# SyncE's row transfers in another order, and the self-attention row after the first search round of its half slot

## The reference, cut to what matters

```
x1 = x  + causal self-attention(LN(x))      16 heads of 32, q and k normed per head
x2 = x1 + cross-attention(LN(x1), ctx)      keeps the 32 largest of 512 scores per row and head
y  = x2 + MLP(LN(x2))                       512 -> 2048 -> 512, int8-like activations, ternary weights
```

## Time and profile before

| | |
|---|---|
| median of 3 runs | 3952.01 us (3951.01 to 3952.15) |
| the profiled execution | 3955.8 us |
| its span, first to last instruction | 3954.0 us |
| mean granted TensorE clock | 0.86 of full speed |
| busy share: TensorE, VectorE, ScalarE, GpSimd | 84%, 81%, 62%, 48% |

### The profile page before, as it was taken

How to read it: one execution, slowest core, us unless ns; L and a number is a source line. 1 busy time by engine, 2 the same in 40 slices (tenths; PEclk the granted TensorE clock), 3 DMA queues, 4 the chain that set the end, 5 groups by cost and what they waited for, 6 DMA issues and landing times.

```text
span 3954.0 us, 61337 instructions
## 1 busy us (share of the span) xinstructions
PE 3320.5 (84%) x18502; PEld 2447.8 (62%) x18502; DVE 3219.5 (81%) x7571; ACT 2451.1 (62%) x4921; POOL 1916.0 (48%) x2444
## 2 busy tenths in 40 slices
PE   2587788998989989998989898998999898877765
PEld 1355576766666667666766676766766676555542
DVE  4311199999989999899989898899979998999961
ACT  3343466666766667666866676667766676555533
POOL 0123234446655465546654555445654564355435
PEclk7667888988989989988988898988898898887778
DMA  8112332332222222322222222322232221211100
GB/s 277 50 51 57 98 77 69 81 86 66 71 66 77 66 62 77 97 76 62 78 78 78 70 67 63 84 72 68 78 82 79 73 70 41 62 46 35 33 22 19
DMA packets 167443, 283.04 MB, mean 72 GB/s; under 512 B 40639, under 2 KB 52939, under 8 KB 166606
## 3 DMA queue, kind: packets, MB, share of 16 engines
q1 hardware_dynamic: 160782, 275.98, 25.6%
q10 hardware_dynamic: 6336, 3.15, 0.3%
HBM read 113.27 MB, written 31.46 MB: 37 GB/s over the span
## 4 chain that ended last, share of the span: by engine, by line
DVE 38%; PE 28%; POOL 13%; issue 9%; ACT 5%; SPq 3%; DMA 1%; DVEq 0%; POOLq 0%; ACTq 0%
DVE cW L881 17%; DVE top L876 14%; PE bank L682 6%; PE bank L607 5%; PE bank L654 4%; POOL srs L1147 3%; SPq L513 3%; PE bank L593 2%; POOL hh L1111 2%; DVE smx L1013 2%; PE bank L670 2%; PE bank L635 2%; POOL hh L1115 2%; PE bank L694 2%; PE bank L701 2%
## 5 line engine op out<-in xcount | busy, mean ns | idle before, releaser
L881 DVE MATCH_REPLACE8 cW<-top,cW 128x512 f32<-128x512 f32 x1536 | 1026.3, 676 | 0.0
L876 DVE MAX8 top<-cW 128x8 f32<-128x512 f32 x1536 | 980.8, 680 | 0.0
L797 ACT ACTIVATE PT<-bank 128x512 f32<-128x512 f32 (+3 forms) x1024 | 539.6, 527 | 363.5 <-PE bank L593 359.8
L1168 POOL TENSOR_TENSOR cS<-cS,cW 128x512 f32<-128x512 f32 x512 | 641.7, 1275 | 199.3 <-ACT cW L825 198.8
L607 PE MATMUL bank<-cv,PT 128*128 128x33 f32 x4096 | 589.0, 291 | 113.3 <-ACT PT L797 111.8
L607 PEld LDWEIGHTS bank<-cv,PT 128*128 128x128 f32 x4096 | 559.1, 211 | 148.1 <-ACT PT L797 141.6
L607 PEld LDWEIGHTS bank<-sv,PT 128*128 128x128 f32 x2560 | 404.8, 214 | 81.1 <-ACT PT L797 57.4
L1175 POOL TENSOR_SCALAR cnb<-top 128x2 f32<-128x2 f32 x256 | 49.0, 191 | 807.4 <-DVE top L876 793.1
L593 PE MATMUL bank<-ident,cS 128*128 128x128 f32 x2048 | 352.2, 300 | 82.4 <-POOL cS L1168 82.4
L825 ACT ACTIVATE cW<-cW,cnb 128x512 f32<-128x512 f32 x512 | 347.6, 733 | 118.5 <-DVE cW L881 118.1
L607 PE MATMUL bank<-sv,PT 128*128 128x33 f32 x2560 | 377.0, 282 | 37.2 <-ACT PT L797 36.0
(11 more groups left out here) (151 smaller groups left out, 6105.0 us busy)
## 6 DMA issues: line engine op xcount, KB each, us to landing
sk_stack<-part SPq DMA_DIRECT2D x512, 64.0 KB, 2.0
sq_stack<-part SPq DMA_DIRECT2D x512, 64.0 KB, 2.0
ck_stack<-part SPq DMA_DIRECT2D x512, 64.0 KB, 2.0
cq_stack<-part SPq DMA_DIRECT2D x512, 64.0 KB, 2.0
w_group<-wa_by_group SPq DMA_DIRECT2D x32, 768.0 KB, 4.5
w_group<-wc_by_group SPq DMA_DIRECT2D x32, 768.0 KB, 4.3
feed<-in_x SPq DMA_DIRECT2D x32, 256.0 KB, 3.0
feed<-in_ctx SPq DMA_DIRECT2D x32, 256.0 KB, 3.0
```

What stands on the lines that cost most here:

```text
L797: act.activation(PT[k][:, 0:n], turned_ps[k][:, 0:n], ACT.Copy).then_inc(turned_read, step("turned_read", label))
L876: dve.max(top8[:, j, r, :], src[:]).then_inc(topk, step("topk", (c, r, "max", j)))
L881: dve.match_replace(cW[j][:], top8[:, j, r, :], src[:], REPLACED).then_inc(topk, step("topk", (c, r, "replace", j)))
L1168: pool.tensor_tensor(cS[m % 2][j][:], cS[m % 2][j][:], cW[j][:], ALU.subtract).then_inc(cprob, step("cprob", (m, j)))
```

## The change

SyncE's list is rewritten. In slot s it now does: feed loads, weights, copies, then the x2 store of this slot, the x1 residual load of slot s + 1, the x1 store of this slot, the MLP row store, the x2 residual load of slot s + 1, and last the `xres` load of slot s + 1. On VectorE `self_rows` moves behind ROUND_1 of the second half. No instruction is added or dropped, and no data or arithmetic differs.

```diff
@@ SyncE, per slot
                             load_feed(pending.pop(0))
-                        t = x1_tile(s)
-                        if t is not None:
-                            sp.wait_ge(x1_stats, upto("x1_stats", ("x1", t)))
-                            sp.dma_start(rows(x1_rows, t), xres[:]).then_inc(x1_out, step("x1_out", t, 16))
-                        t = x2_tile(s)
-                        if t is not None:
-                            sp.wait_ge(dve_rows, upto("dve_rows", ("x2", t)))
-                            sp.dma_start(rows(x2_rows, t), x2t[:]).then_inc(x2_out, step("x2_out", t, 16))
-                        t = cross_tile(s)
-                        ...
-                        t = self_tile(s)
-                        ...
-                        for t in mlp_down(s):
-                        ...
                         for at, which, g, before in loads:
                             if at == s:
                                 load_weights(which, g, before)
...
                                 copy_part(unit, j)
+                        t = cross_tile(s)
+                        if t is not None:
+                            sp.wait_ge(dve_rows, upto("dve_rows", ("x2", t)))
+                            sp.dma_start(rows(x2_rows, t), x2t[:]).then_inc(x2_out, step("x2_out", t, 16))
+                        t = cross_tile(s + 1)
+                        if t is not None:
+                            if t:
+                                sp.wait_ge(dve_rows, upto("dve_rows", ("x2", t - 1)))
+                            sp.wait_ge(x1_out, upto("x1_out", t, 16))
+                            sp.dma_start(x1res[:], rows(x1_rows, t)).then_inc(x1res_in, step("x1res_in", t, 16))
+                        t = self_tile(s)
+                        if t is not None:
+                            sp.wait_ge(x1_stats, upto("x1_stats", ("x1", t)))
+                            sp.dma_start(rows(x1_rows, t), xres[:]).then_inc(x1_out, step("x1_out", t, 16))
                         for t in mlp_down(s - 1):
                             store_y(t)
+                        for t in mlp_down(s + 1):
+                            sp.wait_ge(x2_out, upto("x2_out", t, 16))
+                            if t:
+                                sp.wait_ge(y_out, upto("y_out", t - 1, 16))
+                            sp.dma_start(x2res[:], rows(x2_rows, t)).then_inc(x2res_in, step("x2res_in", t, 16))
+                        t = self_tile(s + 1)
+                        if t is not None:
+                            if t:
+                                sp.wait_ge(x1_out, upto("x1_out", t - 1, 16))
+                                sp.wait_ge(x1_norm, upto("x1_norm", (t - 1, 4)))
+                            sp.dma_start(xres[:], rows(x_rows, t)).then_inc(xres_in, step("xres_in", t, 16))
@@ VectorE, per slot
                         top(c, 1, FIRST_MAX)
                         self_maxima(s, 0)
+                        top(c, 1, ROUND_1)
                         self_rows(s)
-                        top(c, 1, ROUND_1)
                         feed_stats_of(s + 1)
```

## The result

The changed kernel takes 3937.4 us (median of 20 runs, 3929.6 to 3948.6); before, timed beside it, took 3957.2 (3945.0 to 3968.1). The ratio is 0.9952, 95% interval 0.9942 to 0.9961: 19 us or 0.48% faster, where 7.6 us were forecast. The profiled execution of after has a span of 3936.6 us, 17.4 less than the 3954.0 of before.

What follows compares the result with a forecast made beforehand. The bound was taken to change by stage, TensorE in the closing slots of batches 2 to 6, VectorE elsewhere. Terms 1.1 + 2.9 + 1.8 + 1.8 = 7.6 us off 3952.0 gave 3944.4 us, range 3939 to 3952.

Steps and rivals of the forecast that it cites:

- Batches 2 to 6: Row's move in the periodic batches: rounds 14 to 16 worth 0, round 17 worth 0.36 us each, 1.8 us in all.
- I take the row nearest to the path, 0.36: Round 17's wait of 1.17 us vanishes, but only 0.36 us passes on to TensorE's wait for the probabilities.
- The bound of 5.9: High end for batches 2 to 6: round 17's 1.17 us passing on whole in five batches.
- GpSimd's multiply in round 15: VectorE's wait for GpSimd's MLP multiply after round 14's row was to grow from 2.60 to 5.1 us: worth 0.
- Batch 1: Row's move in rounds 14 to 18 of batch 1: 2.9 us passed on, bounds 1.2 and 3.7.
- SyncE's order: Batch 0's x1 store issued ahead of two feed loads: 1.1 us; the moves in later batches 0.
- rival 2: Shorter idle keeps TensorE's clock up in batch 0 and behind batch 1's round 18: 10.8 us off, 3941, chance 0.14.
- The bound of 1.14: High end for SyncE's list in batch 0: the x1 store's earlier issue, all reaching TensorE.
- Batch 7: Row's move in batch 7: 2.50 us at first, 1.8 taken after two things catch up, bounds 0.2 and 2.5.
- rival 4: Row frees TensorE's PSUM bank too late in round 16, 0.9 us in five batches, clock may drop: 3974, chance 0.08.
- Rival 1: VectorE the one bound, every filled wait counts in full: 41 us off, 3911, chance 0.04.
- Rival 3: Gains handed back at VectorE's three terms by equally tight second consumers: some 3.5 us remain, 3948.5, chance 0.23.

Runs made afterwards that it cites:

- e8: The row's move in rounds 14 to 16 of batches 2 to 6 alone, against before, SyncE's list as before: 3959.1 us, ratio 1.0003.
- e2: SyncE's new list alone, with VectorE's order as before, against before: 3953.6 us, ratio 0.9985.
- e12: The row's move in batch 1 alone, SyncE's list as before, against before: 3942.0 us, ratio 0.9975.
- e1: VectorE's move alone, in every closing round, SyncE's list as before, against before: 3939.1 us, ratio 0.9950.
- e9: Before with the x1 residual of round 20 loaded in round 19 ahead of the copies, against before: 3956.5 us, ratio 1.0003.

## Why the prediction was wrong, point by point

**Batches 2 to 6: the term that was mis-sized.** "I take the row nearest to the path, 0.36", five times, gave 1.8 us. The step was right as far as it went: rounds 14 to 16 are worth nothing (e8, 1.0003), and the wait in round 19 fell by 0.36 us on average. What failed is that the work behind that wait was put at no change. It ran at the lower clock in before and less so in after. I had written the price down (eight matmuls, 4.44 us or 2.85), and looked for the event in batch 0 and batch 1 only. Round 19 of batches 2 to 6 is such a place too: 4.1 us of idle time, and then `cross_out` at 6.6 us for 3.7. In place of 1.8 us the five batches got 9.6 us shorter: 1.8 by the wait, 4.8 by the eight matmuls (five times 6.51 less 5.56), and 3.0 that I can't place. By stretches they are shorter by 4.0 between the rows of rounds 16 and 19, 3.6 from 19 to 20, 1.1 from 14 to 16 and 0.9 in the rest. The bound of 5.9 was too low for the same reason: it took a wait of 1.17 us to be worth 1.17 at most.

One reading of the step was wrong without harm: GpSimd's multiply in round 15 does come earlier when VectorE does, by 1.6 us (the wait grew to 3.52, not 5.1). That this is worth nothing too is shown by e8, not by the argument given for it.

**And it depends on what comes before.** Two kernels without the row's move in these batches run them 7 and 9 us faster than the first trace of before, and are 6 and 10 us faster when timed: e2, which has only SyncE's other order in them, and e12, which leaves them alone. In batches 2 to 5 of e12 the wait in round 19 is 4.3 us and the matmuls behind it take 6.0 to 6.1; in before it is 4.1 and 6.6 in three of these batches, 4.3 and 6.1 in the fourth. So there the faster matmuls stand behind the longer gap, and its length alone does not decide the clock behind it. Part of the 9.6 is thus not paid for by anything done in these batches. How much can't be read off two traces, since each execution is one draw, and the kernels' times overlap in part: the parts of the change sum to more than the whole (10 for batch 1 and 13 for batches 2 to 6 against 20 for both, with batches 0 and 7). What decides how long a batch runs stays open, and with it how much of the change's gain is the clock in round 19.

**Batch 1.** Forecast 2.9, measured 3.4 in e1 and e12 up to round 20, inside the bounds; up to round 14 of batch 2 it is 4.8, outside them. In after it is 2.7 from round 15 to 20, with the row of round 14 moving about by 2.4 us on its own (as in e9, which doesn't touch it).

**SyncE's order.** Forecast 1.1, from the issue alone. In batch 0 after and e2 gain 4.1 us from round 15 to round 15 of batch 1, of the twelve traces with the list unchanged nine stay within 0.2 us there, and three move between a loss of 2.6 and a gain of 2.3. Of the 4.1, 1.1 come by the earlier issue, 1.1 by a store that lands faster and 1.6 by the clock, which is rival 2's term; 0.3 are not placed. The bound of 1.14 was too low: what a transfer takes also depends on what is queued right ahead of it. The later batches' moves were rightly priced at 0: no transpose waits for a feed's load there in the traces, though e2's batches 2 to 6 also run shorter than before's, as the table shows, for a reason that stays open.

**Batch 7.** Forecast 1.8, measured 0.6 (529.9 us in after and e1, 530.4 or 530.5 in six kernels without the move there; the others without it took 533.2 to 536.6, so 0.6 is a difference that timed runs can't show). TensorE waits for the row's bank in round 16, and only in this batch:

```profile
3351.06 0.66 PE L635 MATMUL bank<-ident,hh 128*128 128x128 f32 x4 [1.58 <-DVE xres L937]
...
3353.44 1.09 PE L635 MATMUL bank<-ident,hh 128*128 128x128 f32 x4
...
3356.83 0.64 PE L635 MATMUL bank<-ident,hh 128*128 128x128 f32 x4
```

That is rival 4's mechanism, on a small scale. The clock drops behind it, as rival 4 says, for about 3 us: four transposes at 3353.44 take 1.09 us, four of the same kind at 3356.83 only 0.64. I had seen that the row frees the bank no sooner here, and priced the lead that remained at "less than a microsecond" plus the 0.86 of the earlier trace rows; what remained was the first part only.

**The rivals.** Rival 2 (shorter idle, higher clock) comes closest, with too few places: 3.2 us, where the matmuls alone show 6.4 (4.8 in batches 2 to 6, 1.6 in batch 0) and the traces some 9 beyond the waits. It is seen in the traces, and not isolated by a run. Rival 1 counted every wait in full, and its direction for rounds 14 to 16 is refuted by e8. Rival 3 (handed back) is true of batch 7 alone. Rival 4 is true of batch 7 alone.

**My tests.** I wrote that I am wrong if a periodic batch changes by over a microsecond: they changed by 1.9 on average. And if TensorE waits for line 937 in round 16: it does, in batch 7.

## What to carry to other kernels

Where TensorE is waited for, a gap ahead of its work can cost twice: the gap, and the work behind it at the lower clock. A change of a microsecond ahead of it can come back several times over, so look at the granted clock behind every gap on the path, not only at the gap. Filling such a gap with work that nobody reads is a cheap test and here gave as much as the change, and two such fills and the change together twice as much; where another engine is the bound, such a fill gave nothing. And before a few microseconds are put down to an edit, compare the batches that the edit does not touch: here their lengths differed by some 4 us from trace to trace.

## What the runs showed of the hardware

- The same 2283 matmuls of a batch took 392.6 us in one run and 387.2 in another at nearly the same other work, and the batch 433.5 or 430.1 us. Each length persisted for three batches in a row.
- Transposes of the identity alone, put into a gap, raised TensorE's granted clock: 0.85 to 0.93 for 0.70 to 0.78 in the 23 us around round 19 of batches 2 to 6. It was not held up behind them in every batch: the eight matmuls that follow took 3.70 to 6.74 us. The Trainium skill (TensorE: Matmul & The Clock Gate, section HAM oscillation — how this bites in real kernels) says that gaps between bursts bring the clock down again; the fills agree.
- In round 16 of batch 0 a row store landed in 2.3 us with nothing ahead of it in the queue but copies, and in 3.4 to 3.7 behind two feed loads (issue to the issue of the load that waits for it).
- The stretch ahead of the first row, which no kernel here changes, took between 389.1 and 398.4 us.
